# Moving the variance, root and split chain to GpSimd, and half of the final additions to ScalarE and GpSimd

## What is computed

```python
x = x + tanh(g_xattn) * (ctx @ Wv @ Wout + bout)   # what the masked attention comes to
h = layernorm(x); h = layernorm(h) * ln1_g + ln1_b
h = gelu(quant(h) @ quant(w1).T + b1)          # 256 -> 1024
h = layernorm(h) * ln2_g + ln2_b
x = x + tanh(g_ffn) * (quant(h) @ quant(w2).T + b2)   # 1024 -> 256
```

## Time and profile before

| | |
|---|---|
| median of 3 runs | 404.12 us |
| the profiled execution | 403.77 us |
| its span, first to last instruction | 401.9 us |
| VectorE busy | 328.1 us, 82% of the span |
| TensorE busy | 309.3 us, 77% |
| ScalarE busy | 277.6 us, 69% |
| GpSimd busy | 220.9 us, 55% |
| rows copy of round 0 / 15 / last | 52.87 / 356.83 / 391.40 us |

### The profile page before, as it was taken

One profiled execution on the slowest core, in us unless ns is written; L12 is line 12 of the kernel. 1 busy time (PEld: TensorE's weight loads), 2 busy tenths in 40 slices (PEclk: granted clock), 3 DMA queues, 4 the chain that ended last, 5 costly groups with the idle time before them and its releaser, 6 DMA issues.

```text
span 401.9 us, 5821 instructions
## 1 busy us (share of the span) xinstructions
PE 309.3 (77%) x1690; PEld 189.8 (47%) x1690; DVE 328.1 (82%) x794; ACT 277.6 (69%) x446; POOL 220.9 (55%) x118
## 2 busy tenths in 40 slices
PE   2887586969797978888888888888879675848465
PEld 2675344435555555545454546464636342515143
DVE  0489237979999999999999999999999995968781
ACT  1214456869787878796969696969696967879340
POOL 4021163949292929393948484848484757565500
PEclk9999698969999999999999999999999996969688
DMA  7774413336282829191919282828170717252625
GB/s 226 231 238 172 131 52 81 104 58 133 74 208 76 214 66 223 55 229 59 229 60 213 76 195 95 182 106 174 62 155 31 140 44 114 72 111 73 157 55 155
DMA packets 97687, 51.56 MB, mean 128 GB/s; under 512 B 86536, under 2 KB 88769, under 8 KB 97655
## 3 DMA queue, kind: packets, MB, share of 16 engines
q1 hardware_dynamic: 96758, 51.14, 49.9%
q10 hardware_dynamic: 896, 0.04, 0.1%
HBM read 21.78 MB, written 8.41 MB: 75 GB/s over the span
## 4 chain that ended last, share of the span: by engine, by line
DVE 41%; PE 35%; issue 9%; POOL 7%; ACT 3%; DMA 3%; DVEq 0%; POOLq 0%; SPq 0%; ACTq 0%
DVE y L683 10%; PE bank_f L951 8%; POOL rstd L320 6%; PE slot_c L913 5%; DVE res L733 5%; DVE h L642 5%; DVE amax L650 5%; PE slot_a L939 4%; DVE amax L687 3%; PE bank_q L892 3%; PE slot_b L939 3%; DMA c_in<-in_ctx 3%; DVE x L599 3%; DVE parts L585 2%; PE slot_a L936 2%
## 5 line engine op out<-in xcount | busy, mean ns | idle before, releaser
L336 POOL TENSOR_TENSOR y<-u,g_bc 128x1024 f32<-128x1024 f32 x64 | 150.2, 2368 | 27.8 <-DVE parts L585 25.4
L320 POOL TENSOR_TENSOR rstd<-var,half_neg 128x8 f32<-128x8 f32 x18 | 29.5, 1641 | 99.1 <-DVE var L724 88.1
L683 DVE TENSOR_TENSOR y<-y,slot_c 128x1024 f32<-128x1024 f32 x64 | 77.6, 1212 | 5.3 <-PE slot_c L913 5.3
L687 DVE TENSOR_REDUCE amax<-y 128x1 f32<-128x1024 f32 x64 | 78.1, 1220 | 2.2
L427 ACT ACTIVATE q<-y,s 128x1024 f16<-128x1024 f32 x64 | 69.8, 1139 | 9.9 <-DVE s L714 9.8
L454 ACT ACTIVATE junk<-u,usum 128x1024 bf16<-128x1024 f32 x64 | 73.7, 1151 | 1.2
L951 PE MATMUL bank_f<-w2T,q2T 128*128 128x256 f16 x512 | 68.1, 281 | 2.0 <-DVE res L733 2.0
L892 PE MATMUL bank_q<-wvo,ctxT 128*128 128x256 f32 x240 | 64.6, 401 | 0.0
L951 PEld LDWEIGHTS bank_f<-w2T,q2T 128*128 128x128 f16 x512 | 51.4, 101 | 16.6 <-DVE res L733 2.9
L913 PE MATMUL slot_c<-ln_rows,rows 128*128 128x512 bf16 x128 | 41.5, 408 | 16.9 <-DVE y L683 8.4
L418 ACT ACTIVATE q<-h,s 128x256 f16<-128x256 f32 x64 | 27.3, 496 | 37.6 <-DVE s L674 37.5
(11 more groups left out here) (115 smaller groups left out, 407.9 us busy)
## 6 DMA issues: line engine op xcount, KB each, us to landing
c_in<-in_ctx SPq DMA_DIRECT2D x16, 512.0 KB, 3.3
x_in<-in_x SPq DMA_DIRECT2D x16, 512.0 KB, 4.2
out<-res SPq DMA_DIRECT2D x32, 256.0 KB, 2.6
y<-in_L_ffn_w SPq DMA_DIRECT2D x2, 1024.0 KB, 9.6
u<-in_L_xattn_Wkv SPq DMA_DIRECT2D x1, 1024.0 KB, 6.7
u<-in_L_xattn_Wout SPq DMA_DIRECT2D x1, 1024.0 KB, 10.4
q2T<-q SPq DMA_TRANSPOSE x64, 3.3
g_bc<-in_L_ffn_ln_g SPq DMA_DIRECT2D x1, 512.0 KB, 4.3
```

The source lines that it names most:

```text
L320: nc.gpsimd.tensor_tensor(rstd[:, :, :], var[:, :, :], half_neg[:, :, :], ALU.pow) \
L336: nc.gpsimd.tensor_tensor(y[:, k % 2, t, :], u[:, t, :], g2_bc[:, :], ALU.mult).then_inc(gain2_done, 1)
L683: nc.vector.tensor_tensor(line, line, slot_c[:, :], ALU.add).then_inc(y_done, 1)
L687: nc.vector.tensor_reduce(amax2[:, t:t + 1], y[:, k % 2, t, :], AX.X, ALU.max, apply_absolute_value=True).then_inc(amax2_done, 1)
```

## The change

The chain moves: `variance`, `deviations` and `split` are written for GpSimd, between the gains, and the root of round i+1 comes at the end of round i. Of the four finals of a set two stay on VectorE; for tiles 2 and 3 ScalarE copies the second product out of PSUM with its scale (`evict`), and GpSimd adds x1 (`add_residual`). The steps of both scales become one chain of six on 8 columns (`scales`). `rows`, `rstd`, and the scales d get a second buffer. The second half of a set's attention goes into slot b from set 3 on. Pieces change their places on each engine. The diff, cut to its core:

```diff
@@ buffers
+        scaled = sb("scaled", [P, 2, D])
+        rstd = sb("rstd", [P, 2, 2, T])
+        d12 = sb("d12", [P, 2, 2, T])
-        rows = sb("rows", [P, 2, P], BF16)
+        rows = sb("rows", [P, 2, 2, P], BF16)
@@ def attention_bank(k, h):
-            if h == 1 and k < 2:
+            if h == 0:
+                return bank_q[:, :]
+            if k < 3:
                 return slot_c[:, 512:1024] if k == 0 else bank_f[:, :]
-            return bank_q[:, :]
+            return slot_b[:, 0:512]
@@ GpSimd
+                def add_residual(k):
+                    wait(pool, evicted, k + 1)
+                    wait(pool, stored[k % 2], 32 * (k // 2))
+                    nc.gpsimd.tensor_tensor(res[:, k % 2, 2:4, :], scaled[:, :, :],
+                                            x1[:, k % SETS, 2:4, :], ALU.add).then_inc(added, 1)
+                def variance(k):
+                    wait(pool, square_done, T * k + T)
+                    wait(pool, std_done, i + 2)
+                    wait(pool, split_steps, split_count(i))
+                    nc.gpsimd.tensor_scalar(stat[:, 2, :], usum[:, :], -1.0 / H, None, ALU.mult)
+                    nc.gpsimd.tensor_scalar(var[:, 1, :], usq[:, :], 1.0 / float(H) ** 3, LN_EPS,
+                                            ALU.mult, ALU.add).then_inc(var2_done, 1)
+                def deviations():
+                    wait(pool, rstd_done, i + 2)
+                    wait(pool, split_steps, split_count(i - 1))
+                    nc.gpsimd.tensor_tensor(stat[:, 1:4:2, :], var[:, :, :], rstd[:, i % 2, :, :],
+                                            ALU.mult).then_inc(std_done, 1)
...
+                        op = nc.gpsimd.tensor_copy(
+                            parts_q[:, :, :, 3 * (n // 2):3 * (n // 2) + 3],
+                            value.unsqueeze(3).to_broadcast(shape))
...
+                        op = nc.gpsimd.tensor_tensor(rest[:, :, :], value,
+                                                     parts_q[:, :, :, 3 * (n // 2)], ALU.subtract)
...
-                    gain(i - 1, 2)
                     gain(i - 1, 3)
                 if live(i + 1) and i > -1:
                     gain_first(i + 1)
+                if live(i - 3):
+                    add_residual(i - 3)
                 if live(i):
                     gain(i, 0)
                     gain(i, 1)
+                    gain(i, 2)
+                    variance(i)
+                if -1 <= i + 1 <= S:
+                    root(i + 1)
@@ ScalarE
+                def evict(k):
+                    wait(act, ffn_done, T * k + T)
+                    wait(act, added, k)
+                    for t in (2, 3):
+                        op = nc.scalar.activation(scaled[:, t - 2, :],
+                                                  bank_f[:, D * (t - 2):D * (t - 1)], ACT.Copy,
+                                                  scale=d12[:, (k + 1) % 2, 1, t:t + 1])
+                    op.then_inc(evicted, 1)
@@ VectorE
+                def scales(kinds=slice(0, 2), those=slice(0, T)):
...
+                    wait(dve, rstd_done, i + 2)
+                    wait(dve, split_steps, split_count(i))
+                    nc.vector.tensor_tensor(amax_g[one], amax[one], power, ALU.mult) \
+                        .then_inc(scale_steps, 1)
...
+                    wait(dve, gelu_done, T * i)
+                    wait(dve, evicted, min(i - 2, S - 1))
+                    nc.vector.tensor_tensor(d12[:, i % 2, kinds, those], amax_g[one],
+                                            deq[:, kinds].unsqueeze(2).to_broadcast(shape), ALU.mult)
...
                 if live(i - 2):
                     final(i - 2, 0)
+                    final(i - 2, 1)
@@ TensorE, one round
+                if live(i + 3):
+                    turn_context(i + 3, 0)
+                if i <= S + 1:
                     turn_rows()
+                if live(i - 3):
+                    second_product(i - 3, 2)
                 if live(i - 1):
                     correction(i - 1, 0)
+                if live(i - 3):
+                    second_product(i - 3, 3)
                 if live(i):
                     hidden(0)
...
                 if live(i):
                     hidden(3)
+                if live(i - 2):
+                    second_product(i - 2, 0)
+                    second_product(i - 2, 1)
                 if live(i + 1):
                     shift_first(i + 1)
                 if live(i + 3):
                     attention(i + 3, 0)
+                    attention(i + 3, 1)
```

More of the change, by code:

```diff
@@ L756, in body @@
                 if i == -1:
-                    deviations()
-                    for n in range(5):
-                        split(n)
                     residual(1, 0)
                     statistics(1, 0)
+                    statistics(1, 1)
                     round_weights(1, 1)
                     shift_first(0)
-                    for n in range(5):
-                        first(0, n)
+                    first_max(0)
+                    dve.wait_ge(wscaled, 2)
+                    scales()
                     residual(1, 1)
-                    statistics(1, 1)
+                    statistics(1, 2)
+                    statistics(1, 3)
                     for n in range(4):
@@ L770, in body @@
                     return
-                if live(i - 1):
-                    variance(i - 1)
+                if i == 0:
+                    shift_first(1)
+                    first_max(1)
+                    scales()
+                    residual(2, 0)
+                    statistics(2, 0)
+                    statistics(2, 1)
+                    residual(2, 1)
+                    statistics(2, 2)
+                    statistics(2, 3)
+                    for n in range(4):
+                        join(2, n)
+                    return
                 if live(i + 2):
@@ L775, in body @@
                     statistics(i + 2, 0)
-                if i <= S:
-                    deviations()
-                if i <= S + 1:
-                    for n in range(5):
-                        split(n)
-                if live(i - 3):
-                    final(i - 3, 1)
-                if live(i + 2):
-                    residual(i + 2, 1)
-                    statistics(i + 2, 1)
+                    statistics(i + 2, 1)
+                    residual(i + 2, 1)
+                    statistics(i + 2, 2)
@@ L790, in body @@
                     row_max(i - 1, 1)
+                    if live(i + 2):
+                        join(i + 2, 3)
                     if i == S:
-                        for n in range(4):
-                            second(i - 1, n, slice(0, 2))
+                        scales(slice(1, 2), slice(0, 2))
                     row(i - 1, 2)
                     row_max(i - 1, 2)
+                    row(i - 1, 3)
+                    row_max(i - 1, 3)
                 if live(i - 2):
                     final(i - 2, 0)
-                if live(i - 1):
-                    row(i - 1, 3)
-                    row_max(i - 1, 3)
+                    final(i - 2, 1)
@@ L801, in body @@
                 if live(i + 1):
                     shift_first(i + 1)
-                    first(i + 1, 0)
-                for n in range(4):
-                    if i == S:
-                        second(i - 1, n, slice(2, 4))
-                    elif live(i - 1):
-                        second(i - 1, n)
-                    if live(i + 1):
-                        first(i + 1, n + 1)
-                    if live(i + 2):
-                        join(i + 2, n)
+                if live(i + 1):
+                    first_max(i + 1)
+                    scales()
@@ L814, in _ @@
+                if i == S - 1:
+                    scales(slice(1, 2))
+                if i == S:
+                    scales(slice(1, 2), slice(2, 4))
             for i in bodies:
@@ L932, in hidden @@
                         wait(pe, rows_copied, i + 2)
+                    if t == 1 and i > 0:
+                        wait(pe, x1_done, 2 * min(i + 3, S))
                     wait(pe, gelu_done, T * i + t - 1)
@@ L935, in hidden @@
                         half = slice(512 * n, 512 * (n + 1))
-                        nc.tensor.matmul(slot[:, half], rows[:, t // 2, :], b1_rows[:, t % 2, half],
-                                         start=True, stop=False)
+                        nc.tensor.matmul(slot[:, half], rows[:, i % 2, t // 2, :],
+                                         b1_rows[:, t % 2, half], start=True, stop=False)
                         for k in range(KD):
@@ L997, in body @@
                     hidden(1)
-                if live(i + 3) and i > -3:
-                    turn_context(i + 3, 0)
                 if live(i - 1):
```

350 lines of the change are left out of this document (171 added, 179 removed).

## The result

The changed kernel took 464.16 us (median of four runs, 461.08 to 469.95), the kernel before 404.36 on the same chip. The ratio is 1.149, 95% interval 1.144 to 1.154: 60 us slower, where 402.5 was forecast.

What follows compares the result with a forecast made beforehand. VectorE was taken to bound the kernel before (busy 19.35 of 20.60 us a round), waits the changed one. Start -3.4, twelve rounds -4.4, round 15 +1.2 and end +5.3 sum to -1.3 on 403.77: 402.5 us, range 395 to 416.

Steps and rivals of the forecast that it cites:

- VectorE falls to some 17.2 us: VectorE's busy time in a steady round, 19.35 us before, drops to some 17.2 through the work taken off it.
- its two loops: Cycles setting the round: ScalarE's work plus GpSimd's chain, 20.2 us; and one through VectorE's finals, shift and scales, 20.0.
- the terms named: Work leaving VectorE per round: deviations and split 1.5 us, two finals 0.9, variance and scale steps some 0.1 each.
- its slower rival: GpSimd's split steps cost what a cast of 128 costs or more: at chain 5.0 us, round 21.2, time 415; chance 0.25.
- the layout of the round: Steady round from the rows copy: ScalarE waits 1.1 us before the evicting copies, work ends at 15.8, round 20.2.
- The pair of copies: ScalarE's two evicting copies of 128x256 out of PSUM each round, taken at 0.3 us each.
- The chain: GpSimd behind the last square: variance, root, deviations and split take 4.0 us, bounds 3.25 and 5.0, steps 0.28 to 0.3.
- a sign of being wrong: A cast or subtraction on GpSimd of over 0.35 us start to start would show the prediction wrong.
- rows copy of round 3, against before: Start: round 1 begins 0.7 us later, then rounds of 17.6 and 19.0 against 20.3 each: -3.4 us.
- twelve rounds, 3 to 15: Steady rounds take 20.2 us each where they took 20.57: -4.4 us in all.
- round 15, to the rows copy of round 16: Round without contexts takes 19.2 us where it took 18.04: +1.2 us.
- from there to the end: Late second products at the end, behind turning, set 14 and copies, cost +4 to +6.5 us, taken as +5.3.

Runs made afterwards that it cites:

- E2: Kernel before the change, with only its joins moved between the rows and their maxima: 491.43 us, ratio 1.221.
- E7: Changed kernel with each of the seven joins replaced by a tensor_reduce of the same four columns in the same place: 411.83 us, ratio 1.024.
- E4: Changed kernel, full computation, with the four pieces of join together behind VectorE's first shift: 419.05 us, no ratio.
- E9: E8 with second products and finals of tiles 2 and 3 of set 14 a round earlier, ahead of the last turning: 421.37 us, ratio 1.046.
- E8: E4 with all four finals on VectorE, and second products 2 and 3 behind corrections 0 and 1 on TensorE: 429.0 us, no ratio.
- E6: Changed kernel with its joins as GpSimd instructions behind the addition, full computation: 416.77 us, ratio 1.038.
- E11: E10 with the joins on GpSimd as in E6: 401.73 us, ratio 0.988, which rests on two runs.
- E12: E11 with hidden 2 ahead of the attention of set 2 in round 0: 400.45 us, ratio 0.995.
- E10: E4 with all four finals on VectorE and, in the last two rounds, second products 2 and 3 right behind 0 and 1: 409.46 us, ratio 1.015.
- E1: Changed kernel with its five two-input joins replaced by one-input tensor_scalar, same place and size: 465.67 us, ratio 1.151.

## Why the prediction was wrong

**The step that failed** is "VectorE falls to some 17.2 us". The prediction counted what the change takes off VectorE and put the price of the place of what stays, the seven joins, at nothing, without asking what GpSimd runs beside them; neither of its two loops has a row or a join in it. In the changed kernel VectorE is busy for 23.17 and 23.11 us in the rounds from 218.31 and 243.38. In the order of before the joins stand where GpSimd is idle. The diff moves them between the rows, beside gains. There they cost 5.5 us a round instead of 1.1, and the row behind them holds TensorE. E2 shows the cost without the rest of the change (+89 us), E7 the same order without the cost (-52 us), E4 the full computation with the joins elsewhere (VectorE 17.23 us). The 17.2 itself is in part luck: the terms named (1.5, 0.9, and eight steps of 0.1) leave 16.2 of 19.35. No rival of the prediction had this mechanism: its slower rival put the price on GpSimd's steps.

**With the stalls out, the layout of the round held.** E7 is the changed kernel as the prediction had pictured it, and its round from 211.92 can be laid beside it: first evicting copy at +2.39 (2.5 said), first gelu at +5.20 (5.25), last square done at +15.76 (15.8), after a ScalarE wait of 0.98 before the copies (1.1). ScalarE is busy for 17.39 us (17.4 said), GpSimd for 16.61 (16.7). The pair of copies takes 0.84, 0.73 to the next start (0.6 said). Chain and round:

```profile
227.76 0.23 POOL L357 TENSOR_SCALAR stat<-usum 128x4 f32<-128x4 f32 x1 [1.71 <-ACT junk L521]
...
228.38 1.67 POOL L325 TENSOR_TENSOR rstd<-var,half_neg 128x8 f32<-128x8 f32 x1
...
230.12 0.20 POOL L365 TENSOR_TENSOR stat<-var,rstd 128x8 f32<-128x8 f32 x1
...
231.78 0.29 POOL L380 CAST parts<-rest 128x72 bf16<-128x72 f32 x1
```

**The chain** took 4.39 us from the last square (227.68) to the end of the last cast (232.07), 4.0 said, bounds 3.25 and 5.0: a dependent step costs 0.27 to 0.37 start to start, not 0.28, and the upper end is past the 0.35 that the prediction had named as a sign of being wrong. The round is 20.53 for 20.2. By the Trainium skill's GPSIMD Engine Reference, Performance versus the Vector engine, the chain was to be 5.5 by estimate; the run shows 4.39.

**Start, rounds and end.** E7 also shows what the forecast would have missed without the stalls. The span of the profiled execution is 411.2 us, 9.3 more than before:

| | forecast | E7 |
|---|---|---|
| rows copy of round 3, against before | -3.4 | -0.70 (109.24) |
| twelve rounds, 3 to 15 | -4.4 | +0.09 (356.22) |
| round 15, to the rows copy of round 16 | +1.2 | +3.65 (377.91) |
| from there to the end | +5.3 | +6.26 |

The start missed because the rows copy of round 1 came 2.5 us later than before (0.7 said). The twelve rounds missed because they take 20.58 on the mean, ten of them 20.53, for 20.2: the chain's 0.4. At the end the rows copy of round 17 comes at 395.88, and 15.3 us follow it where 10.5 did; about 6 us are the order of the second products, as E9 shows against E8. So had the joins stood clear, the forecast would still have been some 9 us short of E7's 411.83, though inside its range.

**What the change was worth.** The finals on ScalarE cost time once the joins are clear. E6 and E11 both have the joins on GpSimd, and in rounds 3 to 15 they differ by the finals alone (E11's other edit is at the end): 20.48 us a round on the mean in E6, 19.61 in E11, with gelu 0 at +5.2 for mostly +3.8. No run takes the chain back to VectorE, so what the chain on GpSimd is worth by itself is open; E11 and E12, which keep it, end half a per cent to one under the kernel before.

**The place of the joins and the clock.** E10 and E11 differ by the joins' place alone, 20.65 and 19.61 us a round. The last scale starts 17.9 us after the rows copy in E10 (233.89) and 16.2 in E11 (247.13). Most of this follows the clock: in E10 the rounds from 175.72 and 257.65 have a granted clock of 1.00 behind the rows copy, gelu 0 at +3.8, the first quantisation at +16.9 and a length of 19.5, while most others have 0.50, 4.7 to 5.4, 18.0 to 18.4, and 20.7 to 21.1. Rounds at full clock differ by 0.4 us only, 19.5 in E10 and 19.1 in E11. Why the clock falls in ten of E10's twelve rounds, and in two of E11's, the runs do not show.

## What to carry to other kernels

When an instruction moves, look at what the *other* engine runs at its new place: small VectorE work with two SBUF inputs, or a `tensor_scalar`, beside a long GpSimd elementwise instruction costs the rest of that instruction, while reductions and instructions with one of their two operands in PSUM pass. In a profile this reads as small instructions whose mean is many times their usual length, and whose ends fall on the ends of GpSimd's. The price is not only the wait: in E2 1.1 us of work at a bad place cost 6.7 us a round, since what stood behind it fed TensorE. A neighbour engine's idle time may be what makes a sequence cheap: move the small steps to GpSimd's own gaps, or keep them in those.

## What the runs showed that was not expected

- A `tensor_scalar` of four columns, with one input, waits as well: up to 1.51 us by mean in E1, for 0.16 before.
- The wait ends within 0.04 us of the end of GpSimd's instruction and does not lengthen it: gains of 2365 ns on the mean beside 87 us of standing joins, 2368 before.
- The root, 1.67 us on GpSimd for 8 columns, holds nothing back: VectorE's steps beside it take 0.12 to 0.20.
- Small dependent GpSimd steps cost little more than on VectorE: 0.20 to 0.29 us each for 4 to 72 columns in E7, 0.27 to 0.37 start to start, where the five of the split took 1.25 us from 210.86 to 212.11 on VectorE.
- E10 and E11 differ by the place of seven small steps, and TensorE's granted clock behind the turning is 1.2 GHz in the one (0.50 in the window shown) and 2.4 in the other (1.00). The idle time of TensorE right ahead does not tell them apart: in E10 it was 1.46 us before the context turning and 0.56 before the turning of the rows ahead of the window at 0.50, and 1.46 and 0.57 ahead of the round from 175.72, at 1.00. In E11 it was 0.69 and 0.96 ahead of the round from 250.01.
